# A decoder layer on one core: five groups' queries projected in stage one instead of four, twelve late jobs two to a period

## What is computed

```
x = x + attn(layernorm(x))      # q, k, v = x@W + b; Q, K = elu + 1; out = Q (K^T v) / (Q . sum K)
x = x + xattn(layernorm(x), ctx)  # scores normalised per row, softmax, values, Wout
x = x + ffn(layernorm(x))       # top 2 of 8 experts, gelu(h1) * h2, scaled by the gate, summed per row
```

## Time and profile before

| | |
|---|---|
| median of 3 runs | 1552.33 us (1551.38 to 1553.34) |
| the profiled execution's own time | 1546.13 us |
| its span | 1544.3 us |
| mean granted TensorE clock | 0.969 |
| PE busy | 1443.1 us, 93% |
| DVE, ACT, POOL busy | 631.1, 586.0, 370.3 us |

### The profile page before, as it was taken

One profiled execution on the slowest core, in us unless ns is written; L12 is line 12 of the kernel. 1 busy time (PEld: TensorE's weight loads), 2 busy tenths in 40 slices (PEclk: granted clock), 3 DMA queues, 4 the chain that ended last, 5 costly groups with the idle time before them and its releaser, 6 DMA issues.

```text
span 1544.3 us, 21052 instructions
## 1 busy us (share of the span) xinstructions
PE 1443.1 (93%) x7294; PEld 1208.9 (78%) x7295; DVE 631.1 (41%) x1410; ACT 586.0 (38%) x1001; POOL 370.3 (24%) x368
## 2 busy tenths in 40 slices
PE   6999999999983599999999899999999999999998
PEld 4768777778861487888888788898789888897886
DVE  6635666487775243311342431215441431214211
ACT  4535544367764142312332431234431422224211
POOL 3202222146765302011112112021112112021011
PEclk9999999999985699999999999999999999999999
DMA  9300220237655426221343432026523432035122
GB/s 204 56 0 28 82 110 28 82 102 200 164 120 144 124 79 165 60 34 21 96 143 54 129 89 41 7 48 190 148 83 54 113 104 41 0 54 150 14 41 27
DMA packets 80677, 132.46 MB, mean 86 GB/s; under 512 B 31954, under 2 KB 32082, under 8 KB 79604
## 3 DMA queue, kind: packets, MB, share of 16 engines
q1 hardware_dynamic: 63956, 97.67, 22.5%
q0 software_dynamic: 16672, 34.16, 12.0%
HBM read 93.90 MB, written 37.91 MB: 85 GB/s over the span
## 4 chain that ended last, share of the span: by engine, by line
PE 80%; POOL 4%; issue 4%; DVE 4%; DMA 4%; ACT 3%; ACTq 0%; SPq 0%; DVEq 0%; POOLq 0%
PE pg L963 16%; PE pg L965 15%; PE pg L964 15%; PE pj L963 8%; PE pj L965 8%; PE pj L964 8%; POOL slot_table L605 3%; PE pt L1321 1%; PE pj L1198 1%; DVE w_lo L1384 1%; DMA stage<-w 1%; DMA slot_table<-pack,dest 1%; PE pg L1226 1%; PE pg L1164 1%; DMA out_rows<-ost,etab 1%
## 5 line engine op out<-in xcount | busy, mean ns | idle before, releaser
L963 PE MATMUL pg<-xe_hi,w_hi 128*128 128x512 f32 (+2 forms) x1088 | 394.6, 363 | 21.9 <-issue 12.7
L965 PE MATMUL pg<-xe_hi,w_lo 128*128 128x512 f32 (+2 forms) x1088 | 393.3, 361 | 0.0
L964 PE MATMUL pg<-xe_lo,w_hi 128*128 128x512 f32 (+2 forms) x1088 | 393.2, 361 | 0.0
L1808 DVE TENSOR_TENSOR hp<-gl,pg 128x512 f32<-128x512 f32 (+1 forms) x136 | 87.1, 641 | 605.8 <-ACT gl L916 605.8
L682 POOL DMA_INDIRECT out_rows<-ost,etab x62 | 99.1, 1599 | 783.5 <-ACT ost L943 399.1
L963 PEld LDWEIGHTS pg<-xe_hi,w_hi 128*128 128x128 f32 x1088 | 207.8, 191 | 53.7 <-issue 14.2
L916 ACT ACTIVATE gl<-pg 128x512 f32<-128x512 f32 (+1 forms) x136 | 76.1, 560 | 456.3 <-PE pg L965 456.3
L965 PEld LDWEIGHTS pg<-xe_hi,w_lo 128*128 128x128 f32 x1088 | 207.7, 191 | 28.6
L964 PEld LDWEIGHTS pg<-xe_lo,w_hi 128*128 128x128 f32 x1088 | 207.9, 191 | 28.3
L963 PE MATMUL pj<-w_hi,hg_hi 128*128 128x512 f32 x464 | 183.4, 395 | 0.0
L965 PE MATMUL pj<-w_hi,hg_lo 128*128 128x512 f32 x464 | 180.8, 390 | 0.0
(11 more groups left out here) (235 smaller groups left out, 1970.7 us busy)
## 6 DMA issues: line engine op xcount, KB each, us to landing
stage<-w SPq DMA_DIRECT2D x96, 512.0 KB, 5.0
xr<-x SPq DMA_DIRECT2D x8, 1024.0 KB, 10.0
out_rows<-xr SPq DMA_DIRECT2D x8, 1024.0 KB, 7.4
x_rows<-xn SPq DMA_DIRECT2D x8, 1024.0 KB, 7.4
x_in<-x SPq DMA_DIRECT2D x7, 1024.0 KB, 5.1
late_xT<-xT_hi SPq DMA_DIRECT2D x2, 1024.0 KB, 3.9
late_xT<-xT_lo SPq DMA_DIRECT2D x2, 1024.0 KB, 5.9
xT_hi<-late_xT SPq DMA_DIRECT2D x2, 1024.0 KB, 4.9
```

The source lines that it names most:

```text
L963: nc.tensor.matmul(o, lh, rh, start=start, stop=False)
L964: nc.tensor.matmul(o, lh, rl, start=False, stop=False)
L965: return nc.tensor.matmul(o, ll, rh, start=False, stop=stop)
L1808: v.tensor_tensor(hp[j % 2][:, 0:w], gl[j % 2][:, 0:w], pg[:, 2 + j % 2, 0:w], ALU.mult).then_inc(s_hp, 1)
```

## The change

Five positions make their queries in stage one. The order of the groups becomes 0, 1, 2, 3, 4, 7, 5, 6; the late groups are 5, 6 and 7, with twelve jobs, two to a period in places 0 and 1, and one in the stretch before period 0 and one in period 5. Place 2 is empty everywhere. The turned rows of position 5 alone are spilled and loaded again into buffer 0, in period 1. `qT` has a fifth buffer, and to make room `zrow` moves over the buffer of `vT`, whose first writer on DVE now waits for both stores of the zero rows.

```diff
-ORDER = [0, 1, 2, 3, 6, 7, 4, 5]
-EARLY = 4
-SPILLED = [4, 5]
+ORDER = [0, 1, 2, 3, 4, 7, 5, 6]
+EARLY = 5
+SPILLED = 5
...
+LATE_AT = {(-1, 0): [0], (0, 0): [1], (0, 1): [2], (1, 0): [3], (1, 1): [4], (2, 0): [5], (2, 1): [6],
+           (3, 0): [7], (3, 1): [8], (4, 0): [9], (4, 1): [10], (5, 0): [11]}
...
-    spill = nc.dram_tensor("late_xT", (2, 2, P, KC * GT), F32, kind="Internal").ap()
+    spill = nc.dram_tensor("late_xT", (2, P, KC * GT), F32, kind="Internal").ap()
...
-    zrow = fr("zrow", [P, D])
...
+    zrow = alias("zrow", [P, D], F32, sT_at)
...
-                if p in SPILLED:
+                if p == SPILLED:
...
-                for q in range(2):
-                    if g == q:
-                        sp.wait_ge(s_proj, JA + (q + 1) * KC)
-                        sp.wait_ge(s_spill, 64)
...
+                if g == 1:
+                    sp.wait_ge(s_proj, JA + KC)
+                    sp.wait_ge(s_spill, 32)
+                    for half in range(2):
+                        sp.dma_start(xT[0][half][:].bitcast(F32).rearrange("p k t -> p (k t)"), spill[half]
+                                     ).then_inc(s_reload, 16)
...
-                if s - 2 in SPILLED:
-                    act.wait_ge(s_spill, 64)
+                if s - 2 == SPILLED:
+                    act.wait_ge(s_spill, 32)
...
-                    if s in (2 * KC, 3 * KC):
-                        pe.wait_ge(s_reload[s // KC - 2], 32)
+                    if s == 2 * KC:
+                        pe.wait_ge(s_reload, 32)
...
                 dve.wait_ge(s_xset, 1)
+                dve.wait_ge(s_scat, 16)
+                dve.wait_ge(s_add, 16)
                 v.tensor_scalar(kT[:], pt[0][0:XH, 0:NB * CK], xbk_sb[:], float(D) ** -0.5, ALU.add, ALU.mult)
```

More of the change, by code:

```diff
@@ L57 @@
 LATE = (GROUPS - EARLY) * KC
-LATE_AT = {(-1, 0): [0], (-1, 1): [1], (0, 0): [2], (0, 1): [3], (0, 2): [4], (1, 0): [5], (1, 1): [6],
-           (1, 2): [7], (2, 0): [8], (2, 1): [9], (2, 2): [10], (3, 0): [11], (3, 1): [12], (3, 2): [13],
-           (4, 0): [14], (4, 1): [15]}
+LATE_AT = {(-1, 0): [0], (0, 0): [1], (0, 1): [2], (1, 0): [3], (1, 1): [4], (2, 0): [5], (2, 1): [6],
+           (3, 0): [7], (3, 1): [8], (4, 0): [9], (4, 1): [10], (5, 0): [11]}
 BANK = {s: 0 if place == 2 else 1 for (g, place), jobs in LATE_AT.items() for s in jobs}
@@ L295, in decoder @@
         s_spill = sem("late_xT_stored")
-        s_reload = [sem(f"late_xT_loaded{q}") for q in range(2)]
+        s_reload = sem("late_xT_loaded")
         s_proj = sem("proj_psum_ready")
@@ L414, in _ @@
                     sp.dma_start(x_in[:], x_g[ORDER[p + 1]]).then_inc(s_xin, 16)
-                if p in SPILLED:
+                if p == SPILLED:
                     sp.wait_ge(s_tlo, (p + 1) * KC)
                     for half in range(2):
-                        sp.dma_start(spill[p % 2, half], xT[p % 2][half][:].bitcast(F32).rearrange("p k t -> p (k t)")
+                        sp.dma_start(spill[half], xT[p % 2][half][:].bitcast(F32).rearrange("p k t -> p (k t)")
                                      ).then_inc(s_spill, 16)
@@ L454, in _ @@
                 sp.dma_start(out_g[g], xr[g % 4][:]).then_inc(s_out, 16)
-                for q in range(2):
-                    if g == q:
-                        sp.wait_ge(s_proj, JA + (q + 1) * KC)
-                        sp.wait_ge(s_spill, 64)
-                        for half in range(2):
-                            sp.dma_start(xT[q][half][:].bitcast(F32).rearrange("p k t -> p (k t)"), spill[q, half]
-                                         ).then_inc(s_reload[q], 16)
+                if g == 1:
[4 more added lines that the diff above has]
+                                     ).then_inc(s_reload, 16)
                 sp.wait_ge(s_xn3, (g + 1) * TI)
@@ L1415, in turned_lo @@
                 hi, lo = xT[s % 2]
-                if s - 2 in SPILLED:
-                    dve.wait_ge(s_spill, 64)
+                if s - 2 == SPILLED:
+                    dve.wait_ge(s_spill, 32)
                 for k in range(KC):
```

## The result

The changed kernel takes **1568.44 us** (median of 4 runs, 1565.22 to 1572.46), the kernel before, beside it, 1552.07 us (1551.38 to 1553.34): a ratio of **1.0102, 95% interval 1.0085 to 1.0119**, 16.4 us slower.

What follows compares the result with a forecast made beforehand. PE bounds stage one; in stage two the chain of scores, statistics and exponentials leaves PE waits that cover late jobs. +11.1 - 2.9 + 5.3 = +13.5 us on 1552.33 gives 1565.8 us, range 1556 to 1571.

Steps and rivals of the forecast that it cites:

- Stage one, +11.1: Position 4 gets four more query jobs where PE has no gap, 2.77 us each: 11.1 us slower.
- Spill, reload, zero rows, 0: One spill and one reload fewer and the added wait for the zero rows change nothing; reload between -1 and +2 us.
- Stage two, -2.9: Four late jobs fewer in stage two, two to a period, give back 2.9 us; bounds -4.3 and -0.5.
- I take 21.7 us: Length taken for a two-job period, from period 4 before (21.43 us) and GpSimd's chain with a place-0 sum (21.55).
- The upper bound of -0.5: Stage two's least gain, 0.5 us, if the 0.9 us of both waits came in every period.
- the prediction's own sign of being wrong: Stage two's forecast is wrong if periods 1 to 3 are under 21 us or stay at 22.7.
- Dropping the place-2 sum shortens nothing: In two-job periods GpSimd gains no time, because the place-1 sum waits for the exponentials at the period's start.
- The clock, +5.3: A new 4.2 us PE wait before period 0 brings half clock behind it: 5.3 us slower, between 4.0 and 6.4.
- rival A: No new half-clock stretch before period 0: +8.2 us, 1560.5 us; chance 0.23.
- Rival C: The clock falls also at the ends of two-job periods, up to 4 us a fall: +17.5, 1569.8 us; chance 0.12.
- rival B: Shorter wait into period 6 keeps full clock there and before period 0: +1.8, 1554.1 us, not slower; chance 0.08.
- I leave period 6 as it is: Period 5 still ends in a wait of over 3 us, so period 6 was forecast unchanged.

Runs made afterwards that it cites:

- the repeat: The changed kernel run again unaltered, on another measurement beside the second set of filler kernels: 1562.05 us, ratio 1.0095.
- a_warm2: The changed kernel with unread products on rounded operands (small bf16 ones behind period 6) filling PE's waits in stage two: 1563.05 us, ratio 1.0099.
- the two kernels at full clock: a_warm2, and the kernel before with unread products in PE's waits before period 0 and after periods 4, 5 and 6 (1550.22 us, ratio 1.0010).
- the other pair: a_warm3 and b_warm3, the changed kernel and the kernel before with fillers brought to 256 PE instructions: ratios 1.0096 and 1.0025.
- a_warm3: The changed kernel with the fillers of a_warm2 and 31 more unread products before the experts, 256 PE instructions together: 1568.37 us, ratio 1.0096.
- b_warm3: The kernel before with unread products before periods 0, 5, 6, behind period 6 and before the experts, 256 PE instructions: 1556.14 us, ratio 1.0025.

## Why the prediction was right, and where not

It gave 1565.8 us, 1556 to 1571, and slower at 0.88. The time is 1568.44. The sum came out, but one of its terms was wrong in sign, and that two errors partly cancelled is luck.

**Stage one, +11.1: right.** Position 4 grew by 42.98 - 31.92 = 11.06 us, and by 10.9 where the jobs were added alone. By the 131 ns a matmul of the Trainium skill's "TensorE: Matmul & The Clock Gate", "Back-to-back issue gap", it would have been an estimated 6.3; the trace does not agree with that rule for these load-and-multiply triples, which take 0.23 us a matmul.

**Spill, reload, zero rows, 0: right.** `vT` is written at 73.3 us instead of 72.2, but a turning well ahead of it is already as late (48.75 us for 47.67; in the repeat 48.12, and `vT` at 72.7): the start of an execution varies by that much. DVE's wait for slot writes to land is 0.7 us in stage two, once.

**Stage two, -2.9: wrong, the step "I take 21.7 us".** Period 0 at full clock is 21.11 us in `a_warm2`, where 21.4 stood: right. But two-job periods at full clock are 22.7, not 21.7, so periods 1 to 3 give back nothing and periods 4 and 5 cost more: +1.2 in place of -2.9, by the two kernels at full clock (+2.6 by the other pair), outside the bounds. The upper bound of -0.5 does not follow from its own words either: with 21.43 + 0.9 us in periods 1 to 5 the sum is +0.2. And the prediction's own sign of being wrong came, periods 1 to 3 that "stay at 22.7": none of them is under 22.68 us.

The step took the length from period 4 of before, plus GpSimd's place-0 sum. GpSimd's chain came as forecast, and it was not what bounded the period. POOL's timeline in period 3:

```profile
416.74 0.20 POOL L596 TENSOR_TENSOR shift<-neg,rstd 128x4 f32<-128x4 f32 x1
418.07 0.23 POOL L587 TENSOR_SCALAR sig<-mv 128x4 f32<-128x4 f32 x1 [1.13 <-DVE mv L1625]
```

POOL was ready for sigma at 416.94, 18.0 us into the period, and then waited 1.13 us for the statistics of the scores: 21.55 + 1.13 = 22.68. The step missed that the scores of such a period do not run in one piece. They start 12.05 us into it (before 11.74) and last 4.76 us (before 3.79), so they end 16.8 us into the period (415.75 - 398.94) instead of 15.5 (420.10 - 404.57). From there to the next start it is 22.68 - 16.81 = 5.87 us, the 5.90 of before. Period 4 of before, the row that was taken, still had the sum of place 2 between its slot writes, and no pause. The argument that a place-2 job costs what sticks out was right; that its place would not come free was not seen, and "Dropping the place-2 sum shortens nothing" missed that the pauses of PE were seen only where that sum is gone.

**The clock, +5.3: right in kind, a sum of other parts.** The wait of 4.14 us before period 0 was followed by half rate, as the forecast had it against rival A. But it cost 2.6 us, not 5.3: period 0 is 23.69 us with it and 21.11 without; the late job behind the sums already ran at full rate, where in period 6 the values stood at half rate. Rival C's mechanism came too, if not at every period: behind the waits that end periods 1, 3 and 4 of the changed kernel the clock fell (0.86, 0.93, 0.86), in the repeat behind those of periods 3 and 4 only. And rival B's half came: period 6 has a clock of 0.83 instead of 0.71. Together 6.7 - 2.4 = +4.3 us, by the fillers (+3.0 by `a_warm3` and `b_warm3`). "I leave period 6 as it is" was the other weak step; it and C's falls offset each other. Behind waits of 1.3 to 2.2 us the clock fell in some places and not in others. The Trainium skill, "TensorE: Matmul & The Clock Gate", section "HAM oscillation — how this bites in real kernels", says that waits between bursts make the next burst start cold; the trace agrees behind the wait of 4.14 us.

So 11.1 + 1.2 + 4.3 = 16.6 us, beside the 16.4 of the medians and the 14.6 of the repeat. The forecast of +13.5 was near because the term missed in stage two (4.1 us) was partly made up by the clock (1.0 less). That the 16.6 meets the 16.4 so closely says little: its stage two is that of the repeat's profile (163.05 us; the first profile has 166.59), and behind period 6 single profiles differ too, with 53.08 us to the experts in the first, 49.26 in the repeat and 50.87 before. The price of stage one is sure to a few tenths, the split between jobs and clock to a microsecond or two.

What stays open: why the scores pause. It is shown where, how often and beside what, not why; putting something between POOL's slot writes again, or taking the row scale off POOL, was not tried.

## What to carry to other kernels

Price moved work twice: where it goes, by the engine that is full there, and where it leaves, by a period that was measured without it under the same start; a job that hides under another engine's chain gives nothing back. A hole that opens on PE is not only idle time, since the work behind it may run at half rate. And before a kernel with unread fillers or removed instructions is compared with another, compare a stage that none of them touches.

## What the hardware showed that was not expected

- The time of an untouched loop hung on the number of PE instructions ahead of it: 1020.6 to 1023.1 us with the count of before or 256 more (28 or 29 packets in the queue of instructions), 1025.2 to 1028.1 us with others (33 to 39 packets). The Trainium skill, "Runtime: NRT & Kernel Launch", section "Instruction fetch mechanics", says that instructions come in blocks of 256 and that a taken branch to one outside the two at hand stalls for a fetch. The packets agree; that the fetches are the whole 5 us was argued, not shown.
- A float32 filler of 512 columns ran as two passes, 0.88 us at full clock, nearly four times the 0.23 us of a matmul on the rounded operands; twenty of its records without a pause, 15.76 us, ran at half rate to the end.
- PE's scores paused for 0.2 to 1.0 us, with no wait in the program, and went on at the end of POOL's row scale (27 periods, within 0.13 us), where POOL had made eight slot writes in a row ahead of it. DVE and ACT stood idle around the pause as well, but not together with PE: in period 1 of the changed kernel DVE from 362.02 to 363.00 us, ACT from 363.01 to 364.00, PE from 364.15 to 365.14.
